# Scatter-adds of single tiles in two accumulators, and five reloaded tiles added earlier

## The reference

```python
x = x + _L0_xattn_ref(_layernorm(x, axis=-1), ctx_768, ...)   # 16 heads, LoRA, 77 keys
x = x + _L0_ffn_ref(_layernorm(x, axis=-1), ...)              # 8 experts, top 2, one shared expert, hidden 1024
x = x + _L1_xattn_ref(_layernorm(x, axis=-1), ctx_768, ...)   # 8 heads, 77 keys
x = x + _L1_ffn_ref(_layernorm(x, axis=-1), ...)              # 8 experts, top 2, hidden 256
```

## Time and profile before

| | |
|---|---|
| time, median of 3 runs | 891.41 us (887.4 to 892.5) |
| profiled execution, its own time | 889.59 us |
| its span, first to last instruction | 887.7 us |
| mean granted TensorE clock | 0.968 of full speed |
| DMA, whole execution | 115.93 MB, mean 131 GB/s |
| last product of the experts | starts at 583.40 us |
| setup of the second attention | to 621.88 us, when PE transposes its first tile |

### The profile page before, as it was taken

How to read it: one execution, slowest core, us unless ns; L and a number is a source line. 1 busy time by engine, 2 the same in 40 slices (tenths; PEclk the granted TensorE clock), 3 DMA queues, 4 the chain that set the end, 5 groups by cost and what they waited for, 6 DMA issues and landing times. The chain is left out here.

```text
span 887.7 us, 17837 instructions
## 1 busy us (share of the span) xinstructions
PE 822.5 (93%) x6095; PEld 762.0 (86%) x6095; DVE 667.5 (75%) x1359; ACT 483.7 (54%) x1021; POOL 251.0 (28%) x211
## 2 busy tenths in 40 slices
PE   8999999996979999999999999977899779999977
PEld 6888999996679999999999999955888746989877
DVE  4887999996783458888888879948688768766647
ACT  3653333322555567777777768643455542646543
POOL 8411232231015520233433322220122201523430
PEclk9999999998989999999999999989999997999999
DMA  8990000000303257677767778633000041533334
GB/s 299 291 298 21 1 0 1 0 1 10 145 21 136 96 183 270 236 237 236 233 229 218 209 227 254 179 85 123 1 1 1 1 179 54 167 105 105 114 94 163
DMA packets 60067, 115.93 MB, mean 131 GB/s; under 512 B 8482, under 2 KB 45956, under 8 KB 53220
## 3 DMA queue, kind: packets, MB, share of 16 engines
q1 hardware_dynamic: 48420, 97.48, 33.3%
q0 software_dynamic: 9408, 15.53, 7.3%
q10 hardware_dynamic: 2176, 2.10, 0.7%
HBM read 84.29 MB, written 30.79 MB: 130 GB/s over the span
## 5 line engine op out<-in xcount | busy, mean ns | idle before, releaser
L143 PE MATMUL e_ps_h<-e_xh,e_w1h 128*128 128x256 f32 (+1 forms) x496 | 141.6, 286 | 5.6 <-issue 5.6
L144 PE MATMUL e_ps_h<-e_xl,e_w1h 128*128 128x256 f32 (+1 forms) x496 | 139.2, 281 | 0.0
L145 PE MATMUL e_ps_h<-e_xh,e_w1l 128*128 128x256 f32 (+1 forms) x496 | 138.8, 280 | 0.0
L2134 POOL DMA_INDIRECT accumulated<-m_yo,m_token x39 | 77.9, 1997 | 194.2 <-ACT m_yo L2274 164.8
L143 PE MATMUL e_ps_o<-e_w2h,e_hh 128*128 128x256 f32 x440 | 122.3, 278 | 0.0
L145 PE MATMUL e_ps_o<-e_w2h,e_hl 128*128 128x256 f32 x440 | 121.8, 277 | 0.0
L144 PE MATMUL e_ps_o<-e_w2l,e_hh 128*128 128x256 f32 x440 | 121.8, 277 | 0.0
L2254 ACT ACTIVATE e_hf<-e_ps_h,e_b1s 128x256 f32<-128x256 f32 (+1 forms) x248 | 98.1, 447 | 42.1 <-PE e_ps_h L145 41.8
L1030 POOL TENSOR_TENSOR at_pr<-at_pr,at_inv 128x1168 f32<-128x1168 f32 (+2 forms) x48 | 58.6, 1234 | 212.7 <-DVE at_inv L877 212.7
L143 PEld LDWEIGHTS e_ps_h<-e_xh,e_w1h 128*128 128x128 f32 x496 | 94.8, 191 | 5.9 <-issue 5.9
L144 PEld LDWEIGHTS e_ps_h<-e_xl,e_w1h 128*128 128x128 f32 x496 | 94.9, 191 | 0.0
(11 more groups left out here) (428 smaller groups left out, 2314.7 us busy)
## 6 DMA issues: line engine op xcount, KB each, us to landing
e_w1s<-in_m_w SPq DMA_DIRECT2D x24, 1024.0 KB, 4.9
e_w2s<-in_m_w SPq DMA_DIRECT2D x24, 1024.0 KB, 6.9
slots_in<-zero SPq DMA_DIRECT2D x20, 258.0 KB, 9.5
e_xin<-slots_in SPq DMA_DIRECT2D x16, 258.0 KB
last_slots_in<-zero SPq DMA_DIRECT2D x14, 258.0 KB, 8.4
d_xin<-last_slots_in SPq DMA_DIRECT2D x10, 258.0 KB, 2.8
d_results<-last_results SPq DMA_DIRECT2D x10, 256.0 KB, 5.5
as_wk<-in_a_wk SPq DMA_DIRECT2D x2, 1024.0 KB, 9.1
```

The lines of the kernel that those rows point to most:

```text
L143: nc.tensor.matmul(out, lh, rh, start=start, stop=False)
L144: nc.tensor.matmul(out, lh, rl, start=False, stop=False)
L145: return nc.tensor.matmul(out, ll, rh, start=False, stop=stop)
L2134: nc.gpsimd.indirect_dma_start(out=g.acc[a], out_offset=bass.IndirectOffsetOnAxis(ap=token[:, n, a:a + 1], axis=0), in_=yo[:, q, a, :], in ...
```

## The change

Singles now use the accumulator of their parity, so that tile 17 goes to `acc[1]`, 18 to `acc[0]` and so on (tile 16, the first single, keeps `acc[0]`). From tile 17 on POOL waits for the tile two before, which was the last user of that accumulator, and no longer for the one before. In `second_setup` the first five token tiles of the reload are added among the rests for A, one after each of the rests 3 to 7; then come two before each rest for B as long as there are any, which makes two before the first five, one before the sixth, and none behind it.

```diff
--- before.py
+++ after.py
@@ -660,6 +660,7 @@
             last.then_inc(s_bv, 1)
+        tiles = 0
         for a, (gi, b, k) in enumerate(a_items):
...
             dve.wait_ge(s_ahi, a + 1)
             v.tensor_tensor(g.Al[L.n][:, b, k, keys(gi)], ps_a[:, a % 2, 0:n], g.Ah[L.n][:, b, k, keys(gi)], ALU.subtract).then_inc(s_alo, 1)
-        tiles = 0
+            if a >= len(a_items) - 5:
+                before.add(dve, tiles)
+                tiles += 1
         for i, (b, c0, nch) in enumerate(b_items):
             for _ in range(2):
-                before.add(dve, tiles)
-                tiles += 1
+                if tiles < NT:
+                    before.add(dve, tiles)
+                    tiles += 1
             dve.wait_ge(s_bhi, i + 1)
...
@@ -2128,11 +2132,13 @@
             pool.wait_ge(s_ys, n + 1)
-            if n:
+            if n > PAIRS:
+                pool.wait_ge(s_st[q], stored(n - 2))
+            elif n:
                 pool.wait_ge(s_st[1 - q], stored(n - 1))
             for a in range(rows_of(S + n)):
                 nc.gpsimd.indirect_dma_start(
-                    out=g.acc[a], out_offset=bass.IndirectOffsetOnAxis(ap=token[:, n, a:a + 1], axis=0),
+                    out=g.acc[q if n >= PAIRS else a], out_offset=bass.IndirectOffsetOnAxis(ap=token[:, n, a:a + 1], axis=0),
```

## The result

The changed kernel takes **886.17 us** in the median of 11 runs, the one before 891.19 in as many: the ratio is 0.994, with a 95% interval of 0.9913 to 0.9967. The profiled execution took 887.95 us, with a span of 886.0.

A forecast was written before the change was run, and what follows sets the result against it. PE was busy for 93% of the span, so gains were sought only where it stands still or runs slowly. Transposes 3.7 us earlier plus 1.5 us of clock gave 5.2, taken from 890.2: 885.0 us, whole range 881 to 889.

The forecast's parts named there:

- the forecast's own range: Whole kernel: 883.5 to 886.5 us, given a chance of 0.45.
- signs of being wrong: Last scatter-add landing over 5 us, DVE idle over 1 us between first and last add, or unread products ending after 619.
- The scatter-adds: End of the experts, POOL: last issue 3.48 us earlier, landing in the same 3.8, reload issued at 589.5 instead of 593.00.
- The zeroing: POOL's zeroing of `row` ends by 588.40, so ACT's wait goes and the products for A move forward by 2.16 us.
- The first add: DVE, behind rest 3 for A: starts at about 595.4, after waiting about 0.4 us for the reload's first part.
- DVE's 18.5 us: DVE's work from 595.4, adds, bias rows and rests together; without idling it aggregates at 613.9, 4.6 us earlier.
- The unread products: PE, behind rest 3 for B: end at 618.2 instead of 618.89, with transposes right behind them, 3.7 us earlier.
- The lower bound: Transposes only about 2.2 us earlier, where a slow stretch as long as before falls on PE's products.
- The clock term: First attention scores on PE: the clock stays high without the 2.99 us idle before the transposes, 1.5 us gained, or 0.
- The sum: Transposes 3.7 us earlier plus 1.5 us from the clock, 5.2 us, carried through to the kernel's end.
- The slower case: Rival, chance 0.05: two scatter-adds in flight take as long as a pair, up to 8.9 us; 1.4 us slower, about 891.5.
- POOL's rival: Chance 0.13: DVE's filling of `vbd` holds up POOL's last issue, reload 0.8 us later; gain 4.4, 885.8 us.

The follow-up runs named there:

- e3: Kernel before, with the zeroing of `row` done by DVE behind its filling of `vbd` instead of by POOL; ratio to before 0.9944.
- e5: Changed kernel with three more unread products each before PE's waits ahead of the third and fourth product for B; ratio to before 0.9905.
- e1: Kernel before with the first edit alone: single scatter-adds alternate between the accumulators, adds of the reload stay where they were; ratio to before 0.9963.
- e4: Changed kernel with both edits, but 10 unread products instead of 14; ratio to before 0.9936.
- e2: Kernel before with the second edit alone: five adds among the rests for A, scatter-adds still in one accumulator; ratio to before 0.9979.
- e7: Kernel before with the first edit, three adds (not five) behind rests 5 to 7 for A, and 17 unread products; ratio to before 0.9919.
- e8: First edit, three adds behind the last three rests for A, three unread products before each of two waits in B, 17 at the end; median 882.73 us.
- e6: Kernel before with the first edit alone and 20 unread products instead of 14; ratio to before 0.995.

## Why the prediction was right, and where it was not

The time fell within the forecast's own range, and the path was the one forecast, but one term of the sum was too large, and one of the prediction's own signs of being wrong came true. That sign was unread products that end later than 619: on the time scale of the kernel before they end at 619.5 (+34.6). The terms in turn:

**The scatter-adds.** Forecast: the last issue 3.48 earlier, landing in 3.8. Measured from the start of the stretch: 3.48 (+4.24 to +0.76), and 3.8. The reload, forecast 3.5 earlier, moved by 3.48.

**The zeroing.** Forecast: the bias rows 2.16 earlier, measured 2.16. Its share was not seen for what it is, though. The forecast treats it as one of two effects; e3 shows that it carries most of the first edit, since taking it away also kept the clock up in A.

**The first add.** Forecast at 595.4, which is +10.5; measured +10.56. But it waits 1.63 us where at most half a microsecond was forecast, because the products for A ran at the high clock, which the forecast named as likely and left out of this wait. The start of the add comes from the reload and so did not change; DVE's work behind it hardly did either.

**DVE's 18.5 us.** Forecast: aggregation at 613.9, +29.0; measured +29.38. From the first add to the aggregation it is 18.82 (614.81 less 595.99). In e5, where the waits for ACT's high parts for B are gone, it is 18.20 (613.86 less 595.66). So the work was put 0.3 too high, and the waits, which go with the low clock in B, add 0.6.

**The unread products, the term that was mis-sized.** The forecast let them end 8.3 us behind the start of rest 3 for B, as before, and put the transposes 3.7 us earlier. Rest 3 began at 610.52 - 585.43 = +25.1 (forecast +25.0), but the products ended 9.5 behind it, and the transposes came only 2.5 earlier: the step that failed is that the products behind rest 3 would run as fast as before. The clock was at 0.50 from 608 to 614, where before it was low for 3.4 of the 4 us around 611 (0.58 in the mean, e1's fence of before). What differs ahead of it is PE's idle time: 1.54 us for DVE's first rest for B (604.80), where this row of before has 0.21:

```profile
605.09 0.70 PE L637 MATMUL as_ps_kv<-m_xn,as_vbd 128*128 128x256 f32 x2 [0.21 <-DVE B_low L676]
```

PE is ready for B earlier, and DVE, with adds in hand, is not. Both kernels wait another 1.47 us for the second rest. The lower bound given for this case was 2.2. e4 shows that these products are what the transposes wait for, and e5 that the idle time in B makes them late: filled, the transposes come 5.0 earlier than before. The four kernels whose gap is 1.53 to 1.65 (the change, e2, e4, e7) all have the long low stretch, and the two that fill the gaps (e5, e8) have none.

Idle time alone doesn't give the clock, though. In A of the change, e2, e4 and e5 PE idles for 2.27 to 2.56 us, longer than any gap in B, and the clock stays at 1.00 there. And e3 waits 0.55 and then 1.47 us in B, e1 and e6 less, 0.21 and 1.47; yet e3 stays at 1.00, while e6 falls to 0.50 (as does e1, from 606 to 609). First e3's gap and its clock, then e6's clock:

```profile
603.82 0.70 PE L637 MATMUL as_ps_kv<-m_xn,as_vbd 128*128 128x256 f32 x2 [0.55 <-DVE B_low L676]
...
604.00:612.00 8.00, 5.92 (x23) 3.79 (x24) 7.72 (x20) 2.73 (x5) 0.00 (x0) 1.00 0.75 239
```

```profile
609.00:612.00 3.00, 3.00 (x8) 2.43 (x8) 2.90 (x8) 0.59 (x2) 0.00 (x0) 0.50 0.01 3
```

So filled gaps kept the clock up wherever it was tried, but which open gap makes it fall is not settled by its length in these runs.

**The clock term.** Forecast 1.5, measured 3.63 - 2.09 = 1.54; e6 isolates it with 1.28. In the three profiles with 2.99 to 3.81 us of idle time ahead of the transposes (before, e1, e3) the scores are slow; in the seven with 0.52 or less they are not. So at this place the clock went with the idle time in every profile. Each kernel has one profile only, so they can't show whether it varies between executions of one kernel, which the forecast had held possible by the Trainium skill's rule on the gate's own schedule (TensorE: Matmul & The Clock Gate, What's actually happening). That e3 and e6 differ in B the wrong way round agrees with that rule, without showing it.

**The sum.** Forecast 3.7 + 1.5 = 5.2; in the stretch 2.51 + 1.54 = 4.05 of the 4.08 (the rest lies between transposes and scores). The medians are 5.0 us apart, with 2.9 to 7.8 in the interval, so both agree with it, and the absolute time, 885.0 forecast and 886.17 measured, missed by 1.2. Of this, 1.0 is the starting point (890.2 taken, 891.19 measured). That the medians come so near the 5.2 is luck: the stretch, where both edits act, gives 4.1, since the unread products' term was 1.2 too large.

**The rivals.** POOL is not held up: the issue at 586.19 begins 0.43 into DVE's filling of `vbd` (585.76 to 587.10), which was there first, and takes 1.56. So by the trace this filling is not the kind of operation that the Trainium skill (SBUF — State Buffer, SBUF: two separate sides) has in mind. The slower case is out too, for two single scatter-adds in flight take 3.8 each. Nor do long landings need two in flight: in the kernel before, the singles at 550.18 and 557.95, each alone, take 7.0 and 7.8 us to land while the DMA engines move 267 and 358 GB/s. The last three take 3.7 to 3.9 at 35 or 36 GB/s. The two singles between take 5.2 at 49 GB/s and 4.8 at 29, so traffic may be a part of it and not the whole; what made the last pair take 8.9 stays open. The 2.39 us issue at 557.95, from which POOL's rival had its price, ran beside a CAST of 128x2048 on DVE (557.70 to 558.92), a different operation from this filling.

**What the prediction did not ask** is whether the second edit is worth anything on top of the first. In the stretch it costs 1.0 us (e1 against the change). Its first call stands ahead of the second bias rows and waits there for the reload, and PE idles 2.56 us behind it; and with PE waiting in B too, the clock falls there for longer. Moving the calls behind rests 5 to 7, with three more unread products, gives back 1.4 (e7), keeping the clock up 2.45 (e5). With both it is worth 0.9 (e8 against e6). The first edit alone with the gaps in B filled was not run; but in e6 DVE works without a stop from its first add, 15.76 us as before, and PE waits for it ahead of the transposes, so a higher clock in B had little to give there.

## What to carry to other kernels

Look at what stands in the queue behind a serial chain of waits. Here a small zeroing that another engine needed, not the transfers themselves, held most of the gain of shortening the chain.

When work is moved into the idle time of an engine in a fixed order, put it behind the point where its data has surely landed; too early it holds up all that follows. And in a stretch where the engines mostly wait for each other, follow TensorE's clock as a cost of its own: filling gaps with unread products gave 2.5 us where the moved adds had cost 1.0, but as they run in order, too many of them delay the product that is waited for.

## What was not expected of the hardware

Landing of the scatter-adds of tiles 20 and 21 in the kernel before, each alone:

```profile
DMA to landing us min/median/max: 3.7/3.7/3.7
DMA to landing us min/median/max: 3.9/3.9/3.9
```

The accumulating scatter-add of 128 rows of 256 took 3.7 to 3.9 us at the end of the experts, and 3.8 with another one started 2.70 us before it, into the other accumulator. It is no constant: further up, with the DMA engines moving 267 and 358 GB/s, single ones took 7.0 and 7.8.

POOL restarted 0.73 us after the second of these (584.55 + 3.9 = 588.45, then 589.18), but 0.27 after ACT's last instruction. So each link of POOL's chain costs about half a microsecond more than the landing alone. SP's rows show no such delay: the reload starts at 593.00, 0.02 after the last landing at 592.98.
